# Layer 2's layer norms on Trainium2: the scaling by -1/64 moved into the centring instruction

## What is computed

```
def _L0_gnn_ref(inp, adj, W_w, W_b, a):
...
    return jnp.where(h_prime >= 0, h_prime, NEG_SLOPE * h_prime)

def _L1_gnn_ref(x, graph, Wh, bh, Wo, bo, gamma, beta):
    def _gat_layer(h, mask, b):
        scores = jnp.einsum('...nd,...md->...nm', h, h)
        scores = jnp.where(mask, scores, NEG)
        attn = jax.nn.softmax(scores, axis=-1)
        return jnp.einsum('...nm,...md->...nd', attn, h) + b
...
    h2 = jnp.einsum('bnk,dk->bnd', z, Wo)
    out2 = _gat_layer(h2, mask[None], bo)
    z2 = jax.nn.leaky_relu(out2, negative_slope=0.2)
    mu = jnp.mean(z2, axis=-1, keepdims=True)
    var = jnp.mean(jnp.square(z2 - mu), axis=-1, keepdims=True)
    out = (z2 - mu) * jax.lax.rsqrt(var + LN_EPS) * gamma + beta
    return out
x = _layernorm(x + _L0_gnn_ref(x, adj, ...), axis=-1)
x = _layernorm(x + _L1_gnn_ref(x, adj, ...), axis=-1)
```

## Time and profile before

| | |
|---|---|
| runs | 3283.33, 3285.74, 3295.19 us; median 3285.74 |
| the profiled execution | 3288.88 us, of which the span is 3287.0 us |
| mean granted TensorE clock | 0.966 of full speed |
| PE busy | 2949.7 us, 90% of the span |
| DVE busy | 2692.0 us, 82% |
| POOL busy | 2629.1 us, 80% |
| ACT busy | 2273.3 us, 69% |
| DMA queue q1 | 507.32 MB, 80.1% of 16 engines |

### The profile page before, as it was taken

How to read it: one execution, slowest core, us unless ns; L and a number is a source line. 1 busy time by engine, 2 the same in 40 slices (tenths; PEclk the granted TensorE clock), 3 DMA queues, 4 the chain that set the end, 5 groups by cost and what they waited for, 6 DMA issues and landing times. The chain is left out here.

```text
span 3287.0 us, 124182 instructions
## 1 busy us (share of the span) xinstructions
PE 2949.7 (90%) x49399; PEld 2173.3 (66%) x49399; DVE 2692.0 (82%) x5392; ACT 2273.3 (69%) x2542; POOL 2629.1 (80%) x1463
## 2 busy tenths in 40 slices
PE   5856699999999999999999999999996689999990
PEld 3425577777777777777777777777765556666660
DVE  5764588888888888888888888888877779999997
ACT  2146577777777777777777777777765567777776
POOL 1136598999999999899989999999987878888880
PEclk8989999999999999999999999999998989999995
DMA  5207888999999988998999999989977568988872
GB/s 207 70 1 257 232 159 150 156 171 165 156 161 171 162 157 161 167 164 155 161 165 164 158 160 166 167 156 161 171 123 185 179 141 148 159 154 156 145 135 84
DMA packets 1442513, 514.23 MB, mean 156 GB/s; under 512 B 1359054, under 2 KB 1416844, under 8 KB 1439884
## 3 DMA queue, kind: packets, MB, share of 16 engines
q1 hardware_dynamic: 1442060, 507.32, 80.1%
HBM read 105.27 MB, written 66.06 MB: 52 GB/s over the span
## 5 line engine op out<-in xcount | busy, mean ns | idle before, releaser
L551 POOL TENSOR_TENSOR low<-probs 128x1024 f16<-128x1024 f32 x1280 | 2396.6, 1895 | 331.6 <-ACT probs L829 232.2
L829 ACT ACTIVATE probs<-scores,shifted_max 128x2048 f32<-128x2048 f32 x640 | 1282.5, 2004 | 254.2 <-DVE shifted_max L1038 248.0
L696 PE MATMUL ps<-operands 128*128 128x512 f16 x2560 | 974.4, 381 | 12.9 <-DVE neg_max L1033 7.0
L697 PE MATMUL ps<-operands 128*128 128x512 f16 x2560 | 973.9, 380 | 0.0
L1033 DVE CUSTOM_DVE_ANT_0 scores<-ps,mask 128x1024 f32<-128x1024 f32 x640 | 781.7, 1221 | 207.6 <-PE ps L697 200.0
L842 ACT COPY probsT<-ps 128x1024 bf16<-128x1024 bf16 x640 | 647.4, 1012 | 425.2 <-PE ps L705 421.0
L1033 DVE CUSTOM_DVE_ANT_0 scores<-ps,mask,neg_max 128x1024 f32<-128x1024 f32 x640 | 821.8, 1284 | 132.2 <-issue 83.9
L705 PEld LDWEIGHTS ps<-ident,probs 128*128 128x128 bf16 x10240 | 650.7, 98 | 408.2 <-issue 240.9
L705 PE MATMUL ps<-ident,probs 128*128 128x128 bf16 x10240 | 781.7, 219 | 46.0 <-DVE probsT L1045 39.3
L715 PE MATMUL ps<-v_parts,probsT 128*128 128x64 f16 x10240 | 684.7, 193 | 1.3 <-issue 1.3
L716 PE MATMUL ps<-v_parts,probsT 128*128 128x64 f16 x10240 | 685.1, 193 | 0.0
(11 more groups left out here) (144 smaller groups left out, 1829.9 us busy)
## 6 DMA issues: line engine op xcount, KB each, us to landing
operands<-hT_d SPq DMA_DIRECT2D x40, 512.0 KB, 4.5
operands<-hT_d SPq DMA_DIRECT2D x80, 256.0 KB, 4.4
v_parts<-h_d SPq DMA_DIRECT2D x40, 512.0 KB, 4.4
probsT<-low SPq DMA_TRANSPOSE x1280, 3.6
z_d<-outs SPq DMA_DIRECT2D x38, 512.0 KB, 3.2
scores<-in_adj SPq DMA_DIRECT2D x16, 1024.0 KB, 4.8
h_d<-probs SPq DMA_DIRECT2D x32, 512.0 KB, 3.5
hT_d<-probs SPq DMA_DIRECT2D x32, 512.0 KB, 2.8
```

The source lines that it names most:

```text
L551: pool.tensor_tensor(low[:, u, w], probs[:, u, w], high[:, u, w], ALU.subtract).then_inc(sem(f"low{half}"), 1)
L696: pe.matmul(ps[:, b, :], hi_lo[:, p, t * P:(t + 1) * P], hi_lo[:, p, w], start=True, stop=False)
L697: scored = pe.matmul(ps[:, b, :], hi_lo[:, p, t * P:(t + 1) * P], lo_hi[:, p, w], start=False, stop=True)
L829: act.activation(probs[:, 1 - u, :], scores[:, 1 - u, :], ACT.Exp, bias=shifted_max[:, 1 - u:2 - u], scale=-1.0, accum_out=row_sum[:, held ...
```

## The change

In the loop the four sums are no longer multiplied in place by an instruction of their own. The centring instruction, until now a `tensor_tensor` addition with the PSUM tile as first operand and the broadcast mean as second, becomes a `scalar_tensor_tensor`: (sum broadcast over the features) times -1/64, plus the PSUM tile. The sums are now its first tensor operand and the PSUM tile its second. The last stage has the same edit, with 128x1024 elements in SBUF. The semaphore and the wait between the removed and the following instruction go too. Nothing else is different. Line numbers are 2 lower behind line 1081 and 4 lower behind line 1149; the loop's new centring is line 1079, the last stage's line 1145.

```
-                    mean = ln[:, 0, k % 2 * 4:k % 2 * 4 + 4]
+                    total = ln[:, 0, k % 2 * 4:k % 2 * 4 + 4]
                     dve.wait_ge(sem("n_leaky"), n)
-                    dve.tensor_reduce(mean, by_tile(group_bank(k)), AX.X, ALU.add).then_inc(sem("n_sum"), 1)
+                    dve.tensor_reduce(total, by_tile(group_bank(k)), AX.X, ALU.add).then_inc(sem("n_sum"), 1)
                     dve.wait_ge(sem("n_sum"), n)
-                    dve.tensor_scalar(mean, mean, -1.0 / D, None, ALU.mult).then_inc(sem("n_mean"), 1)
-                    dve.wait_ge(sem("n_mean"), n)
-                    dve.tensor_tensor(by_tile(group_bank(k)), by_tile(group_bank(k)), over_four(mean), ALU.add).then_inc(sem("n_centred"), 1)
+                    dve.scalar_tensor_tensor(by_tile(group_bank(k)), over_four(total), -1.0 / D, by_tile(group_bank(k)), ALU.mult, ALU.add).then_inc(sem("n_centred"), 1)
...
                 dve.tensor_reduce(ln_of(3, b), by_tile(x1), AX.X, ALU.add).then_inc(sem("n_sum2"), 1)
                 once(dve, "sum2", b + 1)
-                dve.tensor_scalar(ln_of(3, b), ln_of(3, b), -1.0 / D, None, ALU.mult).then_inc(sem("n_mean2"), 1)
-                once(dve, "mean2", b + 1)
-                dve.tensor_tensor(by_tile(x1), by_tile(x1), over_features(ln_of(3, b)), ALU.add).then_inc(sem("n_centred2"), 1)
+                dve.scalar_tensor_tensor(by_tile(x1), over_features(ln_of(3, b)), -1.0 / D, by_tile(x1), ALU.mult, ALU.add).then_inc(sem("n_centred2"), 1)
```

## The result

The changed kernel takes 3256.34 us (median of 4 runs, 3251.63 to 3261.52) against 3286.6 us for the kernel before (median of 4, 3283.33 to 3295.19). The ratio is 0.9908, with a 95% interval of 0.9883 to 0.9933. It is faster by 30 us at the medians, and by 22 to 38 us by the interval. The profiled execution took 3259.82 us, its span 3258.0 us.

The account below looks back on a forecast made before the run. DVE was taken to bound the second attention, at 17.64 us per group of four tiles. Loop 33.0 + last executions 0.2 + last stage 1.7 - given back 2 = 33 us saved: 3253 us, range 3245 to 3264.

Parts of the forecast that it names:

- The wait inside line 1079: Loop's small scaling on DVE is held until POOL's running instructions end; removing it saves 33.0 us over thirty groups.
- Step C: Third of four tile steps in a second-attention group, between DVE's c=0 masks; falls from 5.42 to 4.27 us.
- DVE would stay the bound by 0.4 us: Second attention: DVE still slower than PE's 16.1 us a group, by 0.4 us instead of 1.5.
- The 0.20 us wait in step A: First tile step of a group: DVE's c=1 starts 0.20 us later than the usual gap; stays, with nothing added.
- step D: Fourth tile step of a second-attention group, between starts of DVE's c=0 masks; 3.76 us before the change.
- PE's wait for the copy: Second attention: PE's wait for DVE's line 1045 shrinks from 1.26 us to a few tenths, in more steps than one.
- The new instruction costs no more than the old: Loop centring: fused form taken as no change from 432 ns; at most 1.0 us more over thirty groups.
- upper bound of 464: Loop centring: 464 ns for 256 elements, from a line through two rows, 32 more than line 1081's 432.
- The last stage, 1.7 us: Last stage: eight removed scalings of 0.174 us plus a gap of 0.04 each save 1.7 us.
- Given back: 2 us: Second attention: PE's formerly hidden waits for transposing DMAs (line 688) show, 4.8 us at most, 2 taken.
- The first two: Loop centring waits for POOL: as the old scaling did, saving 8 us, chance 0.07; or longer, +48 us, chance 0.03.
- The third: Second attention: PE's small delays and DVE's long steps add up, 11 us lost, gain 24 us, 3262 us; chance 0.13.

Follow-up runs that it names:

- the second series: The changed kernel, unaltered, timed again in more rounds against the kernel before: 3264.51 us beside 3290.16, ratio 0.9910.
- the last experiment: Changed kernel; in the second attention ACT adds the constant to the maximum, the small reciprocal moves to where DVE waits for PE: 3256.66 us, ratio to before 0.9892.

## Why the prediction was right, and by how much it was off

The forecast was 3253 us within 3245 to 3264; measured were 3256.3 and, in the second series, 3264.5 beside a kernel before that was slower there as well. Sign and mechanism held. The size did not: my sum gives 33 us, the trace 22.4 to 24.6. That the first median lies only 3 us from the forecast is in part luck: of the 29 us between the two profiled executions, 4.2 lie where nothing was changed.

- *The wait inside line 1079.* Right, and shown by three runs that leave the arithmetic alone: source in PSUM, single elements, POOL short. Removed with the instruction were 0.9 us of waiting and 0.2 of work a group.
- *Step C from 5.42 to 4.27, the group to 16.49.* Measured 4.27 and 16.48. That DVE would stay the bound by 0.4 us is shown by the run that relieved it.
- *The 0.20 us wait in step A stays.* Measured: the idle time ahead of its c=1 is 0.34 instead of 0.37 us, and step D is 0.03 longer in exchange. PE's wait for the copy is now about 0.3 us a group, by the starts of its instructions, where it was 1.26, but most of it falls in one step, not in several as I had written. POOL was busy 89 and 88% of the stage, a little less than the over 90% that I had named.
- *The new instruction costs no more than the old.* Right: 429 ns against 432. My upper bound of 464 wasn't needed, and one support that I gave for it was misread: the line through my two rows gives 715 ns for 512 elements, and the row shows 678.
- *The last stage, 1.7 us.* Measured 1.6 over all profiles.
- *Given back: 2 us.* This is the term that failed. It was 10, 7 in the loop and 3 in the tail, and 12.5 by the second profile of the changed kernel. I had priced one kind of wait, from its mean in the first attention, and halved it. Three things were missing. First, in the kernel before, late arrivals of PE or of a DMA shortened the wait inside line 1079, because POOL had got further by then: PE's pause in tile 113 makes a step of 5.45 us, and the step C behind it takes only 4.48. That cushion went with the wait. Second, POOL and the transposing DMAs are late in the tiles with t = 8 and in the tail: about 4 us, shown by the run without POOL's work, though from one execution. In the tiles with t = 8 alone the three profiles of the new loop have 2.1, 4.1 and 1.0 us more than the kernel before. (The operand loads, which SP issues in the steps 3 to 6, are the likely reason for t = 8; no run tried this.) Third, DVE's own stalls, which change place with the code: 2.7 us in tile 120, and about 0.35 in each of tiles 30, 69 and 101, in all four profiles of the new loop whose code lies unmoved. Tile 14's 1.1 us belong to none of these; they are within its scatter.
- *The rivals.* The first two fell with the constant 429 ns. The third, in which PE's and the DMAs' delays take back 11 us and leave 24, had the size right; I gave it 0.13. Its reason was half right: the DMAs' part was there, PE's was not what I had described. By the sign that I had set for it, a shorter group with the stage not shorter by 30 us, it is this rival that came, though the time lies in the forecast's own range as well.

The medians of 26 to 30 us are larger than what the traces show for the changed stages. The first 2670 us, where the code is the same, scatter by up to 10 us from execution to execution, and the medians are of 4 to 7 runs. I take this for the difference, but haven't shown it.

## What to carry to other kernels

A small instruction whose minimum and median differ sixfold may be waiting inside its own duration, as this one was; look whether its ends coincide with the ends of another engine's instructions before you look for a cheaper operation. Here both forms tried that leave one operand in PSUM were a way out, and for a scaling that stands before an addition the fused form comes free. When you cost a removed wait that ended on another engine's clock, ask what else it absorbed: here about 3/10 of the gain expected before anything is given back didn't arrive, a part of it because of delays that the wait had hidden.

## What the runs showed of the hardware

- A `tensor_scalar` of 128x4 fp32 from SBUF to SBUF waits for POOL (169 to 1795 ns); of 128x1 it does not (141 to 155 ns in 128 executions), nor does one of 128x4 from PSUM to SBUF (160 to 164). Four single instructions beat the one by 0.8 us a group. A `tensor_tensor` of 128x4 with both inputs in SBUF waits (163 to 1779 ns), a `reciprocal` of 128x4 from SBUF to SBUF does not (166 to 170 ns in 160 executions).
- A `scalar_tensor_tensor` with its SBUF operand first and PSUM second, output in PSUM, is as fast as a `tensor_tensor` of the same size, and POOL doesn't hold it (428 to 430 ns in 32 executions).
- DVE stood still for 2.6 us at one place of the program, in each of the four profiles with the same DVE code up to there (2.59, 2.55, 2.59, 2.46 us), and the place changed with 22 instructions put in ahead: 1.9 us even between a mask and its accumulator's read. With the DVE code of the kernel before, tile 119 had a pause of 1.50 us when POOL's work was short, and none or 0.60 us otherwise. PE stood still in tile 113 for 1.05 to 2.16 us and ACT in tile 122 or 123 for 3.0 to 4.8 us in all profiles but the last experiment's, the kernel before among them. Removing or adding instructions can thus shift a few us by this alone. The cause stays open.
